# A two-layer graph network: landing pauses and smaller first batches in layer 1, GpSimd one-hots in layer 2

## What is computed

```python
h = jnp.maximum(_layernorm(x, axis=-1), 0.0)
# layer 1, per edge
c = jnp.concatenate([h[src], h[dst], relation_embedding[edge_type]], axis=1) @ W1 + b1
b = leaky_relu(c @ w2); alpha = softmax of b over the edges with the same dst
x = x + leaky_relu(segment_sum(c * alpha[:, None], dst))
# layer 2
h = jnp.maximum(_layernorm(x, axis=-1), 0.0)
agg = segment_sum(h[src], dst)
x = x + jnp.where((deg > 0)[:, None], agg, h)
```

## Time and profile before

| | |
|---|---|
| median of 3 runs | 1783.18 us (1783.02 to 1783.73) |
| profiled execution, its own time | 1799.49 us |
| its span, first to last instruction | 1795.3 us |
| TensorE busy | 1519.4 us, 85% |
| VectorE busy | 1480.9 us, 82% |
| ScalarE busy | 1335.6 us, 74% |
| GpSimd busy | 1164.3 us, 65% |
| mean granted TensorE clock | 0.949 |

### The profile page before, as it was taken

The page is one execution under the profiler, slowest core; times in us unless marked ns, Lnnn a source line. Parts: engine busy times, 40 slices in busy tenths (PEclk is TensorE's granted clock), DMA queues, the critical chain, the costliest instruction groups (busy, mean ns, idle before and its releaser), DMA issues.

```text
span 1795.3 us, 35038 instructions
## 1 busy us (share of the span) xinstructions
PE 1519.4 (85%) x12139; PEld 1346.7 (75%) x12139; DVE 1480.9 (82%) x4103; ACT 1335.6 (74%) x3492; POOL 1164.3 (65%) x994
## 2 busy tenths in 40 slices
PE   1379999999999999999999982687878778878787
PEld 0269999999999899998999982566656656656566
DVE  5548999999999899999999886677877787787786
ACT  0268888888888788888888952677766777777776
POOL 5756777777767677767777204666666666666661
PEclk9889999999999999999999996899899989989999
DMA  3543666666666566665666454477776677776754
GB/s 105 167 103 102 173 179 168 176 172 180 172 168 177 152 169 175 178 170 151 173 163 169 124 168 134 119 193 190 200 193 179 179 202 193 191 194 188 191 154 122
DMA packets 469368, 298.80 MB, mean 166 GB/s; under 512 B 35662, under 2 KB 438084, under 8 KB 469190
## 3 DMA queue, kind: packets, MB, share of 16 engines
q1 hardware_dynamic: 433942, 243.28, 49.2%
q0 software_dynamic: 35248, 53.28, 11.7%
HBM read 203.78 MB, written 104.34 MB: 172 GB/s over the span
## 4 chain that ended last, share of the span: by engine, by line
PE 47%; ACT 17%; POOL 10%; issue 9%; another core or an unknown queue 6%; DVE 5%; DMA 2%; SPq 0%; DVEq 0%; POOLq 0%; ACTq 0%
POOL xe L1122 8%; PE c_p L1618 5%; PE t_p L1604 5%; PE c_p L1619 5%; ACT an L1527 4%; ACT cs L1544 4%; PE c_p L1621 4%; PE t_p L1601 3%; ACT ae L1530 3%; PE t_p L1606 2%; PE t_p L1605 2%; PE y_p L1637 2%; ACT cs L1549 2%; PE y_p L1634 2%
## 5 line engine op out<-in xcount | busy, mean ns | idle before, releaser
L1112 POOL DMA_INDIRECT xe<-in_x,idx_t x516 | 681.6, 1321 | 264.6 <-issue 163.2
L1122 POOL DMA_INDIRECT xe<-x_d,idx x332 | 335.8, 1011 | 197.0 <-issue 128.2
L1223 DVE BATCH_NORM_STATS2 st<-xn 128x6 f32<-128x256 f32 x843 | 311.4, 413 | 39.4 <-DMA xn<-x_d,idx 27.2
L1527 ACT ACTIVATE an<-xn,nbias,rstd 128x128 f32<-128x128 f32 x783 | 326.9, 483 | 3.1 <-DVE nbias L1257 3.1
L1544 ACT ACTIVATE cs<-xn,nbias,rstd 128x128 f32<-128x128 f32 x782 | 310.3, 479 | 7.1 <-remote 7.1
L1223 DVE BATCH_NORM_STATS2 st<-xe 128x6 f32<-128x256 f32 x446 | 174.6, 412 | 108.0 <-DMA xe<-x_d,idx 96.2
L1530 ACT ACTIVATE ae<-xe,nbias,rstd 128x128 f32<-128x128 f32 x522 | 226.4, 483 | 0.0
L1618 PE MATMUL c_p<-w1a,th 128*128 128x129 f32 x1044 | 218.0, 290 | 9.9 <-issue 9.9
L1562 ACT ACTIVATE cs<-c_p 128x258 f32<-128x258 f32 x261 | 100.2, 384 | 147.6 <-remote 70.6
L1619 PE MATMUL c_p<-w1b,th 128*128 128x129 f32 x1044 | 203.8, 277 | 2.9 <-issue 2.9
L1333 DVE TENSOR_SCALAR sel<-row,plc_t,alpha 128x256 f32<-128x256 bf16 x522 | 194.3, 412 | 3.4
(11 more groups left out here) (207 smaller groups left out, 3667.7 us busy)
## 6 DMA issues: line engine op xcount, KB each, us to landing
xn<-in_x SPq DMA_DIRECT2D x130, 384.0 KB
x_d<-xn SPq DMA_DIRECT2D x130, 384.0 KB
xn<-x_d SPq DMA_DIRECT2D x194, 256.0 KB
out<-xn SPq DMA_DIRECT2D x194, 256.0 KB
plr<-place_d SPq DMA_DIRECT2D x65, 256.0 KB
tyr<-types_d SPq DMA_DIRECT2D x65, 256.0 KB
xe<-in_x,idx_t POOLq DMA_INDIRECT x522
xe<-x_d,idx POOLq DMA_INDIRECT x332
```

The source lines that it names most:

```text
L1112: nc.gpsimd.indirect_dma_start(out=xe_of(u)[:, e, :], out_offset=None, in_=x, in_offset=bass.IndirectOffsetOnAxis(ap=idx_t[:, j:j + 1], ax ...
L1122: nc.gpsimd.indirect_dma_start(out=xe2_of(u)[:, k, :], out_offset=None, in_=x1_d, in_offset=bass.IndirectOffsetOnAxis(ap=idx2[:, j:j + 1], ...
L1223: return v.bn_stats(st[:, j % 2, c:c + 2, :].rearrange("p c t -> p (c t)"), rows_.rearrange("p r d -> p d r"))
L1527: a(an[:, u % 2, i, :], xs_of(u)[:, i, :], ACT.Relu, bias=nbias[:, j % 2, c:c + 1], scale=rstd[:, j % 2, c:c + 1])
```

## The change

1. The batches of the first layer are 2, 2, ten of 4, then 8 (before: 2, 2, 4, 4, then 8).
2. Ahead of the gathers of each third unit in layer 1, GpSimd waits until those of the unit before have landed.
3. In layer 2 the one-hot of the last group of each unit's last tile (128 columns) is made by GpSimd behind the unit's gathers, in one of eight slots of `selT`; VectorE's last instruction of the unit gets 128 columns less. TensorE waits for the new semaphore `last2` before the matmuls that use it.
4. So that the slot is free, GpSimd's wait in layer 2 is for unit u-8 in place of u-7.

```diff
-            LNB, SMB = cut((2, 2, 4, 4) + 30 * (LB,) + (4, 2, 2, 1), LB), cut((), SB_)
+            LNB, SMB = cut((2, 2) + 10 * (4,) + 26 * (LB,) + (4, 2, 2, 1), LB), cut((), SB_)
...
+            last2 = selT[:, :, :, :, :].rearrange("p u e h s -> p (u e h) s")[:, 0:XE2, :]
...
                 def gather(u):
+                    if u % 3 == 0 and u > 0:
+                        pool.wait_ge(gathered.of(u - 1), gathered.count(u - 1))
                     wait(pool, L1.nrm, u - XE + 1)
...
                 def gather2(u):
-                    wait(pool, L2.y, u - XE2 + 2)
+                    wait(pool, L2.y, u - XE2 + 1)
...
+                def select_last2(u):
+                    if u == NU2 - 1:
+                        return
+                    k, first, n, c = spans2(u)[-1]
+                    j = NP2 * k + u // 2
+                    nc.gpsimd.tensor_scalar(last2[:, u % XE2, :], row2[:, (c + n - 1) * P:(c + n) * P], plc2[:, j:j + 1], None, ALU.is_equal
+                                            ).then_inc(s_last2, 1)
...
+                pool.wait_ge(k_row2, 1)
                 for u in range(NU2):
                     gather2(u)
+                    select_last2(u)
...
-                    for k, first, n, c in spans2(u):
+                    for i, (k, first, n, c) in enumerate(spans2(u)):
+                        if i == UT - 1:
+                            n -= 1
...
+                            one = sel2_of(u)[:, at:at + P]
+                            if i == UT - 1 and g == first + n - 1:
+                                pe.wait_ge(s_last2, u + 1)
+                                one = last2[:, u % XE2, :]
```

More of the change, by code:

```diff
@@ L907, in gnn_two_layers @@
             L1, L2 = Layer(1), Layer(2)
+            s_last2 = sem("last2")
             turns, s_own = sem("turns"), sem("own")
@@ L1653, in aggregate2 @@
                         for g in range(first, first + n):
+                            one = sel2_of(u)[:, at:at + P]
+                            if i == UT - 1 and g == first + n - 1:
+                                pe.wait_ge(s_last2, u + 1)
+                                one = last2[:, u % XE2, :]
                             if g < groups2(u):
-                                last = mm(y[:, g // half, g % half * D:(g % half + 1) * D], sel2_of(u)[:, at:at + P], rows_,
+                                last = mm(y[:, g // half, g % half * D:(g % half + 1) * D], one, rows_,
                                           start=False, stop=ends[g] == i, skip_group_check=True)
```

## The result

The changed kernel takes 1955.51 us (median of 4 runs, 1949.72 to 1958.79), the kernel before, measured beside it, 1783.1 us: a ratio of **1.0973 [1.0945, 1.1001]**, slower by 172 us.

A forecast was written before the change was run, and what follows sets the result against it. TensorE bounded layer 1, POOL and the wait at its head layer 2. Pauses +161, layer 1's end -20 and layer 2 -33 made +108 on the profiled 1799.49 us, carried to the median: 1783 + 108 = 1891 us, range 1805 to 1985.

The forecast's parts named there:

- Part 1, TensorE's share and the stream of POOL: Layer 1: POOL becomes the bound with 516 gathers of 1.25 us, gaps and pauses, its last gather 161 us later.
- Some 86% busy: Expected sign in layer 1: TensorE's busy share falls to some 86% as VectorE waits for gathers to land.
- Part 1, the landing: Layer 1: each landing takes 3.0 us (bounds 1.65 and 5.4), so 86 pauses of 3.5 us add 301 us.
- Part 1, no wait for ScalarE left: Layer 1: POOL, being late, no longer waits for ScalarE; before, these waits were 68.2 us in 45 over 700 us.
- a sign that it is wrong: Layer 1: the prediction fails if TensorE is still 97% busy or POOL still waits for ScalarE.
- Part 1, the end of the layer: End of layer 1: TensorE finishes 38 us after POOL's last gather in place of 58.1, giving back 20 us.
- Part 2: Layer 1's batches of 4: nothing on the path; if POOL keeps pace, under 5 us cost or as much saved.
- Part 3: Layer 2: one-hots of 0.5 us on POOL and the earlier wait save 1.1 us a batch of three units, -33 us.
- its list of signs: Signs expected in the changed profile; for layer 2, rare gaps, units of about 6.5 us, POOL one-hots of 0.3 us.
- the stalls of 2 to 3 us at the head of a unit: Layer 2: POOL's stalls on `L2.y`, removed because the wait can be met one unit (6.9 us) sooner.
- +45: Layer 2 if the stalls stay: one-hots cost 1.5 us in each of 30 batches, +45 us in place of -33.
- a third thing as a rival: Layer 2: something else holds TensorE and POOL, so stalls stay: 1969 us; POOL-bound with layer 2 not gaining had 0.2.

## Why the prediction was right, and where its terms were off

Slower was forecast with 0.89, +108 us; measured +172, within the range. POOL did become the bound of layer 1, in the way described. That the time lies within the range is in part luck: its two ends were made with landings of 2.2 and 3.2 us, the measured one is 3.4, and the upper end has room for it only because it counts layer 2 as losing, which it did not do there. By the prediction's steps:

- **Part 1, TensorE's share and the stream of POOL.** "Some 86% busy" was 690 of 800 us, 86%, and VectorE waits for landings as forecast (L1238, 105.5 us in 41 waits). Gathers of 1.25 us were 1.228: 516 x 0.022 = 11 us less than forecast.
- **Part 1, the landing: the mis-sized term.** Taken as 3.0 us, a pause as 3.8 us of idle time; the mean pause was 4.29. 84 x 0.49 = 41 us more. Together 1122 + 41 - 11, less two pauses hidden behind reads of a table (2 x 3.5 = 7), is 1145 us, measured 1147: last gather at 1188 in place of 1163 (1001.9 + 161). The value was taken from the rows of layer 2, the typical wait of VectorE there; the pauses of layer 1 reach beyond the value of the earlier trace rows, 5.4 us, which had been kept as the bound. The Trainium skill's page "DMA: Bandwidth & Descriptors" (anatomy of one DMA on the GpSimd path) would have 2.15 us; the trace disagrees: the 74 pauses that a landing ended are 309.3 / 74 = 4.2 us long, and less 0.8 us to start again that is 3.4 us on average, from 1.4 to 7.0.
- **Part 1, no wait for ScalarE left.** Wrong: 46.4 us in 14 waits remained of 101.4 us in 61, and 79.8 us in the kernel with pauses alone. The prediction had named such waits as a sign that it is wrong, and the sign was too strict: POOL still reaches the end of its ring at times, but nine of the 14 waits, 44.9 of the 46.4 us, stood at the heads of paused units, where a landing had to be waited for anyway. The mean pause of 4.29 us holds them.
- **Part 1, the end of the layer.** TensorE done 38 us after the last gather: 40.1. -20 us was -18.
- **Part 2.** Nothing: +0.12% alone.
- **Part 3.** The one-hot was taken at 0.5 us (its list of signs says 0.3) and is 0.73, within its bounds. From the first gather of layer 2 to the last, a batch of three units gained (6.83 - 6.64) x 3 = 0.6 us in place of 1.1, the layer 19 us in place of 33. When the changed kernel was run again under stalls, layer 2 was only 3 to 6 us shorter than in kernels that have it as before, so even the 19 us are not a firm size. The reason, "the stalls of 2 to 3 us at the head of a unit", held only where there are stalls. Where there are none, the same edits cost 3.4%, the "+45" of the prediction and a little more. The sum of a part against stalls whose cause was not known should have been kept wider.
- **Sum.** +161 -20 -33 = +108; in the two traces +186 -18 -19 = +149, and 150 was measured between the spans. The medians lie 22 us further apart, since before's trace was above its median and after's below: carrying the difference to the median, as the prediction did, hid that.

**Open.** What makes the stalls. The prediction read them as the wait on `L2.y`, for TensorE's work on unit u-7, with a third thing as a rival. In the trace of before TensorE's last matmuls of unit 41 end at 1412.74 + 2.40 = 1415.14 us, but POOL, which waits for nothing else ahead of unit 48, is idle from 1420.37 until 1422.65:

```profile
1412.74 2.40 PE L1655 MATMUL t_p<-cs,sel 128*128 128x128 f32 x20
```

With batches of 4, on a chip without stalls, unit 9 ends at 1128.96 + 2.84 = 1131.80 us and unit 16 goes on 0.8 us later:

```profile
1128.96 2.84 PE L1655 MATMUL y_p<-cs 128*128 128x128 f32 x24
1132.60 1.55 POOL L1122 DMA_INDIRECT xe<-x_d,idx  x1 [1.86 <-PE y_p L1655]
```

So it is throughout: all 41 gaps of before begin at least 2.4 us after the recorded end of unit u-7, and all 8 gaps of the other kernel end 0.79 us after it. What comes late under stalls is the count on `L2.y` itself. Of its 86 recorded updates in the trace of before 55 stand more than 0.1 us behind any recorded end of a unit, half of these 6.1 us or more; with batches of 4 it is 1 of 99 (the ends of matmuls are modelled in both). That fits an edit that takes gaps away by asking for an older value of the count, without TensorE being any quicker. Why the count comes late is not shown: TensorE itself pauses in the middle of a unit until POOL resumes, so the rival that "both could be held by a third thing" is not excluded. Between 19 and 27% of the engines' semaphore updates have no record in the traces with stalls, at most 0.2% in those without, so the former are also the poorer witnesses. The stalls were there on two of the four occasions and could not be switched on or off. The earlier wait alone and both layer 2 edits with the layer 1 of before were not tried under the stalls, nor the one-hots with the old wait without them.

## What to carry to other kernels

A wait for the landing of the gather just issued costs the whole landing (here 2.2 to 7.8 us of idle time, 4.3 on average), each time, on an engine whose stream runs dry by it: compare that with the slack per period, not with the engine's busy share. Before work is given to an engine that issues gathers, count its floor (gathers x (issue + gap)); once the floor is the period, each ns added is paid in full. And what an edit gains by filling stalls should be measured on more than one chip: here layer 2's two edits cost 3.4% without stalls and were not a loss with them.

## What the runs showed of the hardware that was not expected

- **Landings were longer beside transfers of SyncE.** In the changed kernel's trace, 60 pauses with a DMA issue of SyncE (loads and stores of `x`, tables) between 6 us before and 2 us after the last gather's end last 4.81 us on average, the 24 without one 2.99 us. In its second trace they are 4.64 and 3.11 us (61 and 24 pauses), in that of the pauses alone 4.74 and 2.94 us (62 and 23). No run moved SyncE's transfers, so the cause is argued, not shown.
- **A small elementwise instruction on POOL** (128x128 float32, one input, compare with a column) takes 711 to 755 ns, against 295 ns for the select and 195 ns for the memset of the earlier trace rows.
- **VectorE's one-hots are longer in the kernels that have it.** Groups by form, before and after:

```profile
L1344 DVE TENSOR_SCALAR cs<-th,plc 128x384 f32<-128x384 f32 x132 | 50.0, 420 | 0.0
```

```profile
L1361 DVE TENSOR_SCALAR cs<-th,plc 128x384 f32<-128x384 f32 x132 | 54.3, 452 | 0.0
```

420 ns in before, with pauses alone and with batches of 4, 416 with the earlier wait alone; 446 to 458 in all six traces with POOL's one-hots. The Trainium skill's page "SBUF — State Buffer" (section "Who interferes with whom") says that VectorE and GpSimd exclude one another on a pair of ports for a whole instruction, in certain modes of VectorE's; a mean longer by 30 ns agrees in direction, and no run here shows a single clash. VectorE gains nothing from having 128 columns less a unit: all its one-hots of layer 2 together (L1361, in before L1344) keep it busy 178.8 us in the changed kernel, 167.4 in before.
- **The same kernel differs by 8% between occasions**, 1664 to 1803 us. The three groups had three chips, each met on one occasion only, so chip and occasion can't be told apart. Between the trace of before and that of the kernel with batches of 4 (spans of 1795.3 and 1660.3 us), 79 us of the difference lie in layer 2 (702.3 and 623.4 us), where the first has "remote" waits on POOL and the second none.
